# A two-layer cross-attention and mixture-of-experts kernel: seven edits to the turns, the one-hot tables, the padding rows and the begin of a layer

## What is computed

```python
# x: 4 x 512 x 512, ctx: 4 x 512 x 128, float32
x = x + tanh(g_xattn[0]) * attention(layernorm(x), ctx, ctx)
x = x + tanh(g_ffn[0])   * moe0(layernorm(x))   # 8 experts, top 2, width 256, shared 1024
x = x + tanh(g_xattn[1]) * attention(layernorm(x), ctx, ctx)
x = x + tanh(g_ffn[1])   * moe1(layernorm(x))   # 32 experts, top 6, width 192, shared 384

def attention(q, k, v):              # 32 query heads, 8 key heads, 16 wide
    qh = q.reshape(b, s, KVH, G, D).transpose(0, 2, 3, 1, 4)
    kh, vh = (a.reshape(b, s, KVH, D).transpose(0, 2, 1, 3) for a in (k, v))
    scores = einsum('bkgsd,bktd->bkgst', qh, kh) / sqrt(D)
    out = einsum('bkgst,bktd->bkgsd', softmax(scores), vh)
    return out.transpose(0, 3, 1, 2, 4).reshape(b, s, E)

def moe1(x):
    topk_w, topk_i = top_k(sigmoid(x @ gate_w), 6);  topk_w /= topk_w.sum(-1) + 1e-20
    routed = sum over chosen e of topk_w * ((silu(x @ wg[e]) * (x @ wu[e])) @ wd[e])
    return routed + (silu(x @ sg) * (x @ su)) @ sd
```

## Time and profile before

| | us |
|---|---|
| median of three runs | 2112.01 (2111.17 to 2112.18) |
| profiled execution, its own time | 2109.7 |
| its span in the trace | 2107.7 |
| attention, layer 0 | 0 to 440 |
| feed-forward, layer 0 | 440 to 953 |
| attention, layer 1 | 953 to 1393 |
| feed-forward, layer 1 | 1393 to 2107.7 |

### The profile page before, as it was taken

The page is one execution under the profiler, slowest core; times in us unless marked ns, Lnnn a source line. Parts: engine busy times, 40 slices in busy tenths (PEclk is TensorE's granted clock), DMA queues, the critical chain, the costliest instruction groups (busy, mean ns, idle before and its releaser), DMA issues. The chain is left out here.

```text
span 2107.7 us, 41352 instructions
## 1 busy us (share of the span) xinstructions
PE 1927.7 (91%) x10280; PEld 1259.0 (60%) x10281; DVE 1348.3 (64%) x2581; ACT 1137.2 (54%) x1856; POOL 790.4 (37%) x935
## 2 busy tenths in 40 slices
PE   5999999989999999985999999977878999999997
PEld 2444444444888878862344444344667888888886
DVE  6888888841445445426888888847875455555552
ACT  1777777743322335531777777752214566666663
POOL 3122222125310035543222222125764655655554
PEclk9999999989999999995999999987999999999998
DMA  5322222133111468655322222131015888889985
GB/s 165 87 60 61 58 63 60 41 131 120 50 50 60 140 177 200 132 100 147 105 57 58 62 58 64 44 118 42 1 61 157 191 199 197 201 195 207 206 188 100
DMA packets 99572, 232.51 MB, mean 110 GB/s; under 512 B 17410, under 2 KB 20484, under 8 KB 99460
## 3 DMA queue, kind: packets, MB, share of 16 engines
q1 hardware_dynamic: 61060, 136.71, 22.9%
q0 software_dynamic: 33792, 79.71, 19.5%
q10 hardware_dynamic: 4608, 14.68, 2.1%
...
## 5 line engine op out<-in xcount | busy, mean ns | idle before, releaser
L597 DVE TENSOR_REDUCE maxima<-ring_ps 128x1 f32<-128x512 f32 x1024 | 645.0, 682 | 116.1 <-PE ring_ps L386 115.8
L491 ACT ACTIVATE probs<-score_ps 128x1024 f32<-128x1024 f32 x512 | 494.1, 1019 | 47.4 <-PE score_ps L403 45.5
L386 PE MATMUL ring_ps<-k_turned,q_turned 64*128 64x512 f32 x1024 | 408.1, 477 | 31.9 <-DMA q_turned<-q_lo 13.3
L386 PEld LDWEIGHTS ring_ps<-k_turned,q_turned 64*128 64x128 f32 x1024 | 176.8, 192 | 326.1 <-DVE maxima L597 205.9
L1162 PE MATMUL bank_f<-w_gu_parts_f,xg_T_f 128*128 x1800 | 367.3, 352 | 1.9 <-issue 1.9
L1162 PEld LDWEIGHTS bank_f<-w_gu_parts_f,xg_T_f 128*128 128x128 f32 x1800 | 325.7, 190 | 30.4 <-issue 2.8
L403 PE MATMUL score_ps<-q_turned,k_turned 64*128 64x512 f32 x1024 | 327.1, 451 | 14.5 <-ACT probs L491 14.0
L418 PE MATMUL out_ps<-probs,v_ones 128*32 128x512 f32 x2048 | 274.2, 608 | 0.8 <-ACT probs L491 0.7
L1187 PE MATMUL bank_f<-w_dn_parts_f,hg_T_f 96*128 (+1 forms) x888 | 243.4, 410 | 1.4 <-DVE hg_T_f L1754 1.4
L981 POOL DMA_INDIRECT out_x<-y_tok_f,idx_out_f x111 | 177.0, 1595 | 134.7 <-ACT y_tok_f L1388 97.6
L965 POOL DMA_INDIRECT xg_f<-xh_rows_f,idx_in_f x156 | 159.3, 1021 | 178.2 <-DVE idx_in_f L1642 114.0
...
## 6 DMA issues: line engine op xcount, KB each, us to landing
...
q_turned<-q_hi SPq DMA_DIRECT2D x128, 128.0 KB, 2.6
...
k_turned<-k_hi SPq DMA_DIRECT2D x128, 64.0 KB, 2.1
...
```

The lines of the kernel that those rows point to most:

```text
L386: pe.matmul(ring(k, "max", i), q_turned[rows, slot, h // 2, c * P:(c + 1) * P], k_turned[rows, slot, :], start=True, stop=True).then_inc(m ...
L491: act.activation(probs[:, c % 2, pair, :, :], score_ps[:, pair, :, :], ACT.Exp, scale=float(D) ** -0.5).then_inc(exped, 1)
L597: dve.tensor_reduce(maxima[:, par, col:col + 1], ring(k, "max", i), AX.X, ALU.max).then_inc(max_taken, 1)
```

## The change

In attention:

1. pick becomes a 128 by 128 permutation, and turn_out uses pe.transpose four times. Each writes 128 columns, of which the first 68 count; the next one overwrites the rest. The maxima move to column 332 (MAX_AT) of the bank.
2. TURN_Q_AT goes from 5 to 4 and COPY_Q_AT from 6 to 5: the turn of q and its copy stand one group earlier on PE, ACT and in the ring.
3. In the tail of the layer POOL takes the root (for the next block's layer norm) before it adds the last results to x.
4. At a layer's begin ctx_T of batch 0 is loaded from ACT's queue, ahead of all else there; DVE splits the keys before it normalizes; ACT rounds the first two q tiles straight from the ring's bank, and DVE takes the remainder of both from there.

In the feed-forward:

5. In layer 1 HOTS is 7 in place of 3, one table product comes after every second gate/up product, and none between down products (36 a group as before, all in the gate/up part). HOTS_AHEAD says how many one-hots DVE makes ahead.
6. weights_of takes three ranks at a time (chosen, 128 by 1536), and the second call comes behind the first seven one-hots.
7. The padding has two blocks of 128 spare rows, one for even tiles and one for odd, and the last expert's last tile is no longer marked (memset to 0 at meets[E - 1]).

```diff
-TURN_AT, TURN_Q_AT, INVERT_AT = 2, 5, 8
-COPY_OUT_AT, COPY_TURN_AT, COPY_Q_AT = 1, 3, 6
+HEAD_ROWS = P // G
+MAX_AT = (TPB - 1) * G * USED + P
+TURN_AT, TURN_Q_AT, INVERT_AT = 2, 4, 8
+COPY_OUT_AT, COPY_TURN_AT, COPY_Q_AT = 1, 3, 5
...
                 for c in range(TPB):
-                    mm = pe.matmul(ring(k, "turn")[:, c * G * USED:(c + 1) * G * USED], out_rows[:, c * P:(c + 1) * P],
-                                   pick[:].rearrange("p h e -> p (h e)"), start=True, stop=True)
+
+                    mm = pe.transpose(ring(k, "turn")[:, c * G * USED:c * G * USED + P], out_rows[:, c * P:(c + 1) * P], pick[:])
                 mm.then_inc(out_turned, 1)
...
                 split_q(b, k)
+                if isinstance(b, int) and b == B and k >= 1:
+
+                    root(k - 1, B)
                 add_x(b, k)
-                if isinstance(b, int) and b == B and k >= 1:
-
-                    root(k - 1, B)
...
-            load_ctx_T(0)
...
+            act.dma_start(ctx_T[:, :, 0:S], t["ctx_T"][:, :, 0:S]).then_inc(ctx_T_loaded[0], 16)
...
+            def first_q_hi(pair):
+
+                act.wait_ge(q_turns, pair + 1)
+                act.activation(q_hi[:, 0, pair, :], ring(KVH - 3 + 2 * pair, "q"), ACT.Copy).then_inc(q_copied, 1)
+
             round_k(0)
-            copy_q(-1, 5)
-            copy_q(-1, 7)
+            first_q_hi(0)
+            first_q_hi(1)
...
+            def first_q_lo(pair, signal):
+
+                dve.wait_ge(q_copied, pair + 1)
+                dve.tensor_tensor(q_lo[:, 0, pair, :], ring(KVH - 3 + 2 * pair, "q"), q_hi[:, 0, pair, :].bitcast(F32), ALU.subtract
+                                  ).then_inc(signal, 1)
...
             moments_of_batch(0)
+            for half in range(2):
+                split_k(0, half)
             dve.wait_ge(ln_rstd, 1)
             for c in range(TPB):
                 normalize(0, c)
-            for half in range(2):
-                split_k(0, half)
-            split_second_q()
+            first_q_lo(0, q_split)
+            first_q_lo(1, second_q)
...
-    ROWS = TOK + P
+    ROWS = TOK + 2 * P
 
     PAIRS = TT * K
-    HOTS = min(4, 2 * HC * F // 512)
-    EVERY, DOWN = (4 * HC, 0) if layer == 0 else (3, TPB * FC)
+    HOTS = 4 if layer == 0 else 7
+    HOTS_AHEAD = 2 if layer == 0 else HOTS - 2
+    EVERY = 4 * HC if layer == 0 else 2
+    KS = min(K, 3)
...
-                        if DOWN and g > 0 and hots_by(g, 6 * HC * FC, c * FC + f + 1) <= PAIRS:
-                            table_sum(hots_by(g, 6 * HC * FC, c * FC + f + 1) - 1)
...
-                then(dve.tensor_copy(meets[:, E - 1:E], ones_e[:, 0:1]))
+                then(dve.memset(meets[:, E - 1:E], 0.0))
...
-            for k in range(min(K, 4)):
-                weights_of(k)
+            weights_of(0)
             shared_x_lo(1)
             shared_w_lo(FC, 0)
             shared_w_lo(FC, 1)
-            for k in range(4, K):
+            for k in range(KS, K, KS):
+                tile_one_hots(HOTS)
                 weights_of(k)
```

101 lines of the change are left out of this document (57 added, 44 removed).

## The result

| | before | changed |
|---|---|---|
| median, us | 2111.59 (2106.26 to 2112.18, 4 runs) | 2086.56 (2083.46 to 2092.01, 4 runs) |
| ratio | | 0.989, 95% interval 0.9862 to 0.9918 |
| span of the profiled execution | 2107.7 | 2081.5 |

The change makes the kernel 25 us faster, where 72 were forecast; the time lies above the range of 2020 to 2070. A second set of runs, beside other runs of the kernel before, gave 2089.68 (2085.96 to 2091.14, 4 runs), ratio 0.9888 (0.9872 to 0.9905).

A forecast was written before the change was run, and what follows sets the result against it. PE, busy 91%, was taken as the bound; in attention, DVE bound pairs of groups without a turn, PE those with one. Terms summing to -72.3 took 2109.7 to 2037.4; 2.3 for the median gave 2039.7, predicted 2040, range 2020 to 2070.

The forecast's parts named there:

- transposes: Attention: turning output rows by four transposes saves PE 0.45 us in each of 64 units, all showing: -28.8 us.
- turn of q earlier: Attention: one group earlier ends ACT's 1.60 us idleness; -0.8 us in 22 units, -0.17 in 6: -18.6 us.
- one-hots: Layer 1's shared expert: down parts and group 1's gate/up get shorter, group 2's gate/up 3.6 us longer: -15.3 us.
- batched weights: Feed-forward: larger weights_of does the same elements in fewer instructions, beside PE's work: 0.
- padding: Feed-forward ends: the last scatter no longer waits for the one before to land; 3.1 and 3.5 us, -6.6 in all.
- begin: Layer begin: copies of q leave the chain to the first scores, the earlier key split counts against: -0.5 per layer, -1.0 us.
- one with a turn by PE: Attention: a pair of groups with the output rows' turn is PE-bound at 3.39 us; 2.94 after, still over DVE's 2.7.
- rival F: Attention: DVE becomes the bound in the pair with the turn; half of both attention terms goes; 2064 us, 4%.
- rival A: Attention: transposes overlapping in output columns wait for each other, 1.86 us per four, +52.5; 2121 us, 3%.
- rival D: Attention: each turn by transposes lowers PE's clock, about 3.3 us per unit, +210; 2250 us, 2%.
- rival C: Layer 1's shared expert: POOL bounds gate/up parts, DVE the down parts, so the one-hot change gives nothing; 2055 us, 15%.
- B: Attention: moving the turn of q gives nothing, PE or the ring keeps the 1.14 us; 2058 us, 15%.

The follow-up runs named there:

- e7: Label not spelled out in the text, apparently: changed kernel with DVE's reciprocal one maximum later (INVERT_AT 9); units with a turn of q 12.18 to 12.07 us.
- e9: Label not spelled out in the text, apparently: changed kernel with the output rows turned in group 1, right behind the product with v; 1.0 us per layer gained.
- e13: Changed kernel with ring banks in order of writing, INVERT_AT 9, ctx_T on SP, normalization first and POOL's multiplication late; span 2063.6 us against 2081.5.

## Why the prediction was wrong, step by step

| term | forecast | measured | by |
|---|---|---|---|
| transposes | -28.8 | -6.4 | undone |
| turn of q earlier | -18.6 | -5.6 | undone |
| one-hots | -15.3 | -8.8 | undone, groups 1 to 3 |
| batched weights | 0 | -4.0 | undone, groups 1 to 3 |
| padding | -6.6 | -4.9 to -6.4 | undone, last two scatters |
| root first | -2.0 | -1.5 | last copy to next block, 3.70 to 2.97 us |
| begin | -1.0 | +13.7 | first scores 22.00 to 28.82, layer 1 +6.9 |

The measured terms add up to about -18, where the medians say -25.0 and -22.7 and the two profiled executions -26.2. What is left lies mostly ahead of group 1 in layer 1 (70.1 us before, 67.1 after) and in the expert loop (509.5 and 504.9), stretches that differ by 2.9 and 4.7 us between versions that are the same there; no run assigns it.

**What bounds the kernel.** The step that failed is "one with a turn by PE". It took the pair's 3.39 us as PE's own time, and 3.39 less 0.45 as still above DVE's 2.7, as if the two engines ran apart. So it put 28.8 us where 6.4 came. They are coupled by three banks. With the turn some 0.45 shorter (1.08 to 0.62) PE waits 0.29 more inside the same pair for a bank, as the timeline of the changed kernel shows in the load ahead of its last score product:

```profile
318.50 0.18 PEld L392 LDWEIGHTS ring_ps<-k_turned,q_turned 64*128 64x128 f32 x1 [0.29 <-DVE maxima L607]
318.93 1.06 PE L424 MATMUL out_ps<-probs,v_ones 128*32 128x512 f32 x8
```

The pair from 315.63 to 318.93 takes 3.30, and 0.36 of the 0.45 is lost to DVE. No run gave the ring a fourth bank or DVE's maxima another length; the coupling is shown by the turn lengthened twice, by the orders of e7, e9 and e13, and by the two last units. Here rival F had the mechanism (DVE becomes the bound in the pair with the turn) and gave it 4%, with half of the terms gone, where three quarters went. The price itself was right: the four transposes take 0.62 us in the timeline, as four of q do, with no serialization by overlapping columns (rival A) and a granted clock of 1.00 in the 340 us of attention (rival D), which now hold four more transposes in each unit.

**The turn of q.** The mechanism was right: ACT's idleness before the copy went from 1.60 to 0.90 us. The size was not: 0.45 per light unit in place of 0.8. The cause is put down to the same coupling: moving DVE's reciprocal by one place gives 0.10 in these units, but no run splits up the 0.35 that is missing. The count was off as well: DVE also prepares a batch in 6 units with a turn of each layer, 12 in all and not 6, so 16 are light and not 22. And the step named no cost for units without a turn, although the ring's table is made with the q tile's place in every odd unit. That one could have been read in the code: 0.7 us in each of four units.

**The begin.** The forecast looked only at the chain through DVE, ACT and the transfers. Edit 4 also took split_q(-1, 5) from POOL's list, and so moved the multiplication behind it from 17.57 to 15.02 us, into DVE's normalization. It is the one instruction that no edit names that became the largest cost (5.2 per layer). The bound given for this term, 2.4, rested on the wrong list. The doubt about ctx_T on another queue was justified: 1.7 us lost rather than 0 or a gain.

**The feed-forward.** Down parts were forecast at 17.2 and 19.5 us and took 15.7 both. For the second the forecast took DVE's busy time of before, 19.48 us in 39 instructions, though one-hots leave the part; DVE now has 25 there, in 14.15 us. Group 2's gate/up part was forecast at 25.7 and took 25.2. Group 1's gate/up part was forecast to gain 3.7 and lost 2.8: the first seven one-hots take DVE 0.92 us each, not 0.59, and PE then stands 5.5 us until the eighth, behind the second weights, is ready:

```profile
1451.83 6.43 DVE L1638 SCALAR_TENSOR_TENSOR tile_hot_f<-count_f_f,tile_of_f,entry_f 128x384 fp32r<-128x384 f32 x7
...
1466.88 0.66 PE L1105 MATMUL bank_f<-tile_hot_f,slot_hot_f 128*128 128x384 f32 x1 [5.52 <-DVE tile_hot_f L1638]
```

The batched weights, put at 0, gave 4.0. Root was about right. So was padding in layer 0; the last scatter starts 0.73 us after its source, not 0.35, and in layer 1 the gain is smaller in most traces.

**The signs.** Of the signs of being right, the transposes (0.62 us for four) and the down parts came. The units did not: 11.48 and 12.18 us in place of about 11.1, and 0.70 apart, where at most 0.4 was stated; ACT's idleness before the copy of q is 0.90, not gone. Of the signs of being wrong one came: group 1's gate/up part takes 32.70 us with POOL busy 31.70, which is rival C's mechanism, there alone, with DVE as busy (32.53).

**The chances.** Faster was right, and by more than the bound of 0.2%. The range was too narrow because cases that fell together (F's mechanism, over two thirds of B, a begin that costs) were treated as rare single ones. The first two have one cause, the ring between PE and DVE; the begin's is another, an instruction that moved forward on POOL's list.
